# A decoder's second attention: the rotary jobs' scaling moved from VectorE to ScalarE, the table added in one instruction

## What is computed

```python
q = _layernorm(q, qn_g, qn_b)
k = _layernorm(k, kn_g, kn_b)
cos, sin = _rope_tables(s, D, ROPE_BASE)
q = q * cos + _rotate_half(q) * sin
k = k * cos + _rotate_half(k) * sin
...
scores = jnp.einsum('bhqd,bhkd->bhqk', q, k) / jnp.sqrt(jnp.float32(D))
scores = jnp.where(causal, -jnp.inf, scores)
weights = jax.nn.softmax(scores, axis=-1)
attn = jnp.einsum('bhqk,bhkd->bhqd', weights, v)
```

## Time and profile before

| | us |
|---|---|
| median of 3 runs | 946.5 (942.33 to 947.36) |
| profiled execution: time | 946.95 |
| profiled execution: span of the core | 945.2 |
| score slots 0 to 57 of attention 1 | 365.9 to 683.3 |

### The profile page before, as it was taken

The page is one execution under the profiler, slowest core; times in us unless marked ns, Lnnn a source line. Parts: engine busy times, 40 slices in busy tenths (PEclk is TensorE's granted clock), DMA queues, the critical chain, the costliest instruction groups (busy, mean ns, idle before and its releaser), DMA issues.

```text
span 945.2 us, 11992 instructions
## 1 busy us (share of the span) xinstructions
PE 777.5 (82%) x3984; PEld 563.8 (60%) x3984; DVE 695.0 (74%) x1067; ACT 473.2 (50%) x990; POOL 269.0 (28%) x178
## 2 busy tenths in 40 slices
PE   6761568867898976999988888989883799999997
PEld 2341446654343743676666656666662589999996
DVE  4879699889758977898999769869928644444443
ACT  1653467722255014566676547556763344444442
POOL 1000356522230121011010201201003366666663
PEclk9685679988899999999999989999996899999999
DMA  4313134325020220111111110103000053444341
GB/s 168 120 40 142 67 110 135 112 90 211 3 92 23 90 89 0 45 45 45 46 45 46 45 45 24 66 27 109 2 1 0 7 189 133 141 156 136 133 134 44
DMA packets 24208, 74.60 MB, mean 79 GB/s; under 512 B 3120, under 2 KB 5696, under 8 KB 23776
## 3 DMA queue, kind: packets, MB, share of 16 engines
q1 hardware_dynamic: 23776, 71.51, 21.4%
q10 hardware_dynamic: 384, 2.49, 0.8%
HBM read 72.55 MB, written 1.44 MB: 78 GB/s over the span
## 4 chain that ended last, share of the span: by engine, by line
PE 51%; DVE 20%; ACT 13%; issue 13%; POOL 2%; DMA 0%; POOLq 0%; DVEq 0%; ACTq 0%; SPq 0%
PE ps L1561 8%; PE ps L1675 6%; PE ps L1676 6%; PE ps L1677 6%; DVE hS L917 5%; PE ps L1522 4%; PE ps L1640 4%; ACT dA L544 3%; PE ps L1541 3%; PE ps L1324 2%; PE ps L1628 2%; DVE ps L909 2%; PE ps L1316 1%; PE ps L1619 1%; DVE lnst L939 1%
## 5 line engine op out<-in xcount | busy, mean ns | idle before, releaser
L1324 PE MATMUL ps<-ident,hS 128*128 128x128 f32 x512 | 73.3, 292 | 56.4 <-POOL hS L391 31.1
L1295 DVE SCALAR_TENSOR_TENSOR arena<-ps,arena 128x1024 f32<-128x1024 f32 x32 | 39.2, 1225 | 102.1 <-ACT arena L783 93.1
L917 DVE TENSOR_TENSOR_SCAN hS<-dA,hS 128x1024 f32<-128x1024 f32 x41 | 93.7, 2286 | 23.7 <-ACT dA L544 23.3
L1324 PEld LDWEIGHTS ps<-ident,hS 128*128 128x128 f32 x512 | 62.1, 150 | 77.0 <-POOL hS L391 38.1
L1561 PE MATMUL ps<-WB,hT 128*128 128x512 f32 x192 | 91.6, 623 | 3.8 <-DVE arena L1170 2.0
L419 POOL TENSOR_SCALAR jst<-jst 128x8 f32<-128x8 f32 x20 | 12.3, 613 | 276.7 <-DVE jst L1178 276.7
L391 POOL TENSOR_TENSOR hS<-hS,BCb 128x1024 f32<-128x1024 f32 x23 | 56.1, 2439 | 111.1 <-DVE ps L909 96.1
L544 ACT ACTIVATE dA<-DEL,negA 128x510 f32<-128x510 f32 x128 | 85.0, 720 | 4.7 <-DVE hS L917 4.3
L433 POOL TENSOR_TENSOR MHl<-arena,MHh 128x1024 fp32r<-128x1024 f32 x34 | 81.7, 2404 | 17.0 <-ACT MHh L786 17.0
L1675 PE MATMUL ps<-Wh,MHh 128*128 128x256 f32 x272 | 77.9, 286 | 5.8 <-POOL MHl L433 5.8
L1676 PE MATMUL ps<-Wl,MHh 128*128 128x256 f32 x272 | 77.6, 285 | 0.0
(11 more groups left out here) (223 smaller groups left out, 1885.1 us busy)
## 6 DMA issues: line engine op xcount, KB each, us to landing
BCb<-bc_dram SPq DMA_DIRECT2D x64, 512.0 KB, 3.7
arena<-gate_dram SPq DMA_DIRECT2D x32, 512.0 KB, 3.6
WB<-in_we SPq DMA_DIRECT2D x34, 256.0 KB, 2.7
WB<-in_wqkv SPq DMA_DIRECT2D x1, 3072.0 KB, 12.8
WA<-in_wo ACTq DMA_DIRECT2D x1, 2048.0 KB, 7.6
WA<-in_ffn SPq DMA_DIRECT2D x1, 1408.0 KB, 8.0
pkb<-in_pk SPq DMA_DIRECT2D x2, 698.0 KB, 4.7
X<-in_x SPq DMA_DIRECT2D x1, 1024.0 KB, 7.6
```

Of the source, the lines that this page charges most:

```text
L917: v.tensor_tensor_scan(f(h), f(a), f(dbu(g)), 0.0, ALU.mult, ALU.add).then_inc(s["scan_done"], 1)
L1324: last = mm(ps[:, ACC_BANK + j // 2, 256 * (j % 2) + P * d:256 * (j % 2) + P * d + P], src[:, d, P * j:P * j + P], ident[:], start=(first ...
```

## The change

ScalarE multiplies job_a by the eight scales, in place, as a part of its own, "scale", which stands in rope's slot. VectorE's rope keeps only the addition of job_a and job_b, and a new part, "bias", adds the table to all heads in one instruction of 1024 columns, one slot later (in the first two jobs in the same slot). tr stays where it was. For the jobs (b+1, 1) rope comes two slots after proj instead of three. In the costs rope goes from 3.2 to 1.2 and bias is 1.2. The semaphore job_rope counts jobs, no longer eighths.

```diff
+            def job_scale(b, i):
+                j = JOB[b, i]
+                act.wait_ge(s["job_add"], j + 1)
+                act.wait_ge(s["job_rstd"], j + 1)
+                for t in range(2):
+                    for h in range(REP1):
+                        c = slice(D1 * h, D1 * h + D1)
+                        last = sc.mul(job_a(j)[:, t, c], job_a(j)[:, t, c], jst[:, j % 2, 2, REP1 * t + h:REP1 * t + h + 1])
+                last.then_inc(s["job_scaled"], 1)
...
                 dve.wait_ge(s["job_rot"], 3 * (j + 1))
                 v.tensor_tensor(job_a(j), job_a(j), job_b(j), ALU.add).then_inc(s["job_add"], 1)
-                dve.wait_ge(s["job_add"], j + 1)
-                dve.wait_ge(s["job_rstd"], j + 1)
-                for t in range(2):
-                    for h in range(REP1):
-                        c = slice(D1 * h, D1 * h + D1)
-                        v.scalar_tensor_tensor(job_a(j)[:, t, c], job_a(j)[:, t, c], jst[:, j % 2, 2, REP1 * t + h:REP1 * t + h + 1],
-                                               tabs[:, 3 * x + 2, t, :], ALU.mult, ALU.add).then_inc(s["job_rope"], 1)
+
+            def job_bias(b, i):
+                j, x = JOB[b, i], 0 if i else 1
+                dve.wait_ge(s["job_scaled"], j + 1)
+                heads = job_a(j).rearrange("p t (h d) -> p t h d", d=D1)
+                shift = tabs[:, 3 * x + 2, :, :].unsqueeze(2).broadcast_to([P, 2, REP1, D1])
+                v.tensor_tensor(heads, heads, shift, ALU.add).then_inc(s["job_rope"], 1)
...
             def job_tr(b, i, x):
                 j = JOB[b, i]
-                pe.wait_ge(s["job_rope"], 8 * (j + 1))
+                pe.wait_ge(s["job_rope"], j + 1)
...
-    def rope_job(slot, b, i, rope=3, tr=5):
+    def rope_job(slot, b, i, rope=3, tr=5, later=1):
...
         at(slot + rope, "rope", (b, i))
+        at(slot + rope, "scale", (b, i))
+        at(slot + rope + later, "bias", (b, i))
...
-    rope_job(-8, 0, 0, 2, 3)
-    rope_job(-7, 0, 1, 2, 3)
+    rope_job(-8, 0, 0, 2, 3, 0)
+    rope_job(-7, 0, 1, 2, 3, 0)
...
-            rope_job(u + 9, b + 1, 1, 3, 4)
+            rope_job(u + 9, b + 1, 1, 2, 4)
...
-    cost = {"rot": 2.6, "sum": 1.2, "rope": 3.2, "dbu": 1.2, "scan": 3.5}
+    cost = {"rot": 2.6, "sum": 1.2, "rope": 1.2, "bias": 1.2, "dbu": 1.2, "scan": 3.5}
...
-        plan += pick("wo1", "rope", "rot", "sum") + [p for p in now if p[0] != "da"]
+        plan += pick("wo1", "rope", "scale", "rot", "sum", "bias") + [p for p in now if p[0] != "da"]
```

More of the change, by code:

```diff
@@ L256, in build @@
             s0_mm s0_tanh s0_exp pv0_mm pv0_copied pv0_tr at0_den at0_ready a_tr_mm a_tr_act a_tr_dve o0_mm x_new fsc_ready gate_tanh gate_h gate_mm gate_t nega_exp nega_ready pt0_fill
-            f_mm f_tanh f_hid fd_mm wdn_ready w1_mean w1_centered tabs_ready job_mm job_sq job_rot job_sum job_rstd job_add job_rope
+            f_mm f_tanh f_hid fd_mm wdn_ready w1_mean w1_centered tabs_ready job_mm job_sq job_rot job_sum job_rstd job_add job_scaled job_rope
             job_tr_mm job_tr_copied v_mm v_copied s1_mm s1_max s1_exp s1_rc s1_norm pt1_mm pt1_copied pv1_mm at1_copied o1_mm
@@ L750, in _ @@
                     job_copy(*a)
+                elif kind == "scale":
+                    job_scale(*a)
                 elif kind == "exp":
@@ L1175, in job_sum @@
                 if j >= 2:
-                    dve.wait_ge(s["job_rope"], 8 * (j - 1))
+                    dve.wait_ge(s["job_rope"], j - 1)
                 dve.wait_ge(s["job_sq"], j + 1)
@@ L1215, in _ @@
                     job_rope(*a)
+                elif kind == "bias":
+                    job_bias(*a)
                 elif kind == "max":
```

## The result

The changed kernel takes 976.22 us (median, 974.58 to 977.14) against 946.93 of the kernel before in the same runs: ratio 1.0318, 95% interval 1.0282 to 1.0354, slower. The forecast was 966, range 945 to 984. The profiled execution took 977.14, its span is 975.3. Executions of the kernel before differ among themselves: over all its measurements here they took 941.7 to 949.0, at a mean granted clock between 0.919 and 0.931. So a stage time, which is read from one profiled execution, can be off by a few us.

What follows compares the result with a forecast made beforehand. ScalarE's in-order run, as long as TensorE's own work, was taken to leave no room in the score slots. 33.0 - 13.9 - 1.5 + 4.4 = +22, less 2 or 3 for accumulations, +19: 966 us, range 945 to 984.

Steps and rivals of the forecast that it cites:

- What bounds the stage: Attention 1's score slots: ScalarE's run from projection's end to output copy is as long as TensorE's work, 0.07 us apart.
- The price of a multiplication: ScalarE's eight per job: 0.30 us each overlapped, 2.4 us per job; 3.3 if not overlapped at all.
- VectorE's saving is off the path: VectorE gives back about 1.0 us per job, 20 us; beyond 1.5 us in the last slots, no time gained.
- The exposed slots: Score slots behind a scale: 14 x 2.4 us less 0.49 and 1.09, +32.0, with the tail slot +33.
- The pacing: Planner's new costs remove five of six scan waits for the exp: -13.9 us, plus -1.5 from VectorE in the last slots.
- The accumulations: The scan's accumulations fall oftener in slots where TensorE stands still, taking off 2 or 3 us.
- The prologue: Before the score slots: job 1's scale stands behind the values' copy, its transposes at 361.2 instead of 356.83, +4.4 us.
- The signs that were named: Among others: output-copy wait up some 25 us, L544 waits down to one or two, job 1's transposes at 361.
- The bias: VectorE's bias addition waits for ScalarE's scale near nothing and hides; without cover it would cost up to 1 us a job.
- VectorE as the bound: Faster rival: multiplications fit ScalarE's idle time, 20 us of VectorE leave the path: 927, or 915 without dA waits; chance 0.12.
- The draw by soaking up: Rival: delays vanish where VectorE is late anyway; half of 33 stays, 952, or 947 with two thirds soaked up; chance 0.15.
- The dearer case: Slower rival: dA waits persist in other slots, or bias wait holds VectorE 1 us in most jobs: 989; chance 0.13.

Runs made afterwards that it cites:

- the pair of 941.51 and 945.74 us: Both exps put ahead of the scan: in the kernel before with the new planner costs and slots, 941.51 us; in the changed kernel with scales ahead of the square, 945.74.
- one multiplication: Changed kernel with one of each job's eight multiplications kept, seven blocks unscaled, all waits kept: 943.26 us, ratio 0.9978.
- the new pacing: Kernel before with only the planner's new costs and slots, VectorE keeping the eight scale-and-add instructions: 939.76 us, ratio 0.9935.
- the old costs: Changed kernel with only the planner's cost line put back (rope 3.2, no bias cost): 989.14 us, ratio 1.0486.
- the faster kernels: Split kernels with one multiplication (943.26 us) or early scale and both exps ahead of the scan (945.74), set against old-rope kernels at 939.76 and 941.51.
- the place in the list: Changed kernel with ScalarE's multiplications moved ahead of the square or copy that waits for TensorE: 943.18 us, ratio 0.9979.
- one line of order: Kernel before with one planner line changed, both exps of the next scan step ahead of the scan, old costs: 937.03 us, ratio 0.9905.
- the kernel that has only the prologue mended: Changed kernel with only job 1's scale moved ahead of the value projection's copy in slot -5: 966.06 us, ratio 1.0237.

## Why the prediction was right, point by point

*What bounds the stage: right.* A run of ScalarE as long as TensorE's own work, with 0.07 us between them, was read from one slot; the stall of 2.39 us stands exactly there. The slot was one without an accumulation, the kind with the least room. Of the normalisations behind a scale in the stage, none waits for VectorE any more.

*The price of a multiplication: right.* 2.35 us per job from first start to successor, 2.4 said.

*VectorE's saving is off the path: right, and shown* by the pair of 941.51 and 945.74 us, and by one multiplication at 943.26 against the new pacing's 939.76: less work on VectorE, and no gain.

*The exposed slots: right in kind, sized a little high.* The sum had +33 for the slots, the tail slot included, all of it time in which TensorE stands still. With the old costs the split adds 27.2 us of that. It also adds 8.3 us of busy time at a lower clock, for which the sum had no term: +35.5 together. On top of the new pacing it adds 29.0 (308.5 to 337.5): 19.5 of idle time and 9.5 of busy time.

*The pacing: near in size by luck.* The sum had -13.9 and -1.5. The -13.9 are the scans' waits for the exp, "taken whole". By itself the pacing took 9.0 us off these waits and 8.8 off the stage, yet TensorE's idle time did not fall (36.3 to 36.8). What fell was its busy time, by 9.4, most of it by a higher clock. With the scale on ScalarE the pacing gives -15.4, but that is 8.2 of busy and 7.1 of idle time, and most of the 7.1 are the accumulations. The step "I take it whole, because the stretches of chain around those waits run through the scan" was thus not borne out: the size came out near by other means.

*The accumulations: right in kind, sized too small.* The sum had 2 or 3. Seven more of the exposed slots carry one than with the old costs, and that takes off about 6 us.

*The prologue: mis-sized.* +4.4 was said, with bounds 2 to 5; it was +7.2. The first transposes come 14.68 us after the first projection, against 12.68 before: the 2.0 that was said. The second ones come 26.87 after it, against 21.33: +5.5 where 4.4 was said, because the first transposes and the value projection ran slower after a longer idle time of TensorE (1.97 and 5.72 us against 1.37 and 5.05). The projection behind the second ones took 5.04 us instead of 3.60, after an idle time of 4.70: the granted clock was 0.50 from 365.80 to 368.00, where before it was 1.00 from 356.83 to 361.20. The sum has no term for that. It carried each delay on as its own length and nothing more, and this is the step of this term that failed.

Together: the forecast's +19 was 15 for the stage and 4 for the prologue, and 20.2 and 7.2 were measured. Spans differ by 30.1, because 2.3 more lie ahead of the first projection, where the instructions are the same and the profiles of all kernels here differ by up to 4.1 us, and 0.5 behind slot 58. The medians differ by 29.3. So the mechanism, a stall behind the scale, is the foretold one; that the total came as near as it did owes something to luck, since the clock had no term and the pacing's term stood for something else.

*The signs that were named.* VectorE's waits for L544 are down to two. TensorE's wait for the output copy rose by 18.6 us, not by some 25, as ten of the stalls are partly filled by accumulations. The transposes of job 1 come at 364.63, not at 361.

*The bias: mostly hidden.* VectorE waited 12.9 us for the scale in ten jobs, at most 3.1, where "near nothing" was said; TensorE hardly waited for the bias in the stage. In the faster kernels the split costs some 3.5 to 4 us. Part of the 3.5 is the prologue, and the bias may be a part of both; no run isolates it.

*The rivals.* VectorE as the bound fell with 976. The draw by soaking up fell with the time as well. ScalarE's wait for the reciprocal did fall, but the new pacing alone takes it from 30.5 to 15.1, and behind the scale itself no normalisation waited and TensorE stood still. The dearer case said 989, and the old costs give 989.14; the scans' waits for the exp are indeed kept there (18.8 us), but the forecast's size for it left out the clock. The faster rival's second figure should be 913 by its own terms (947 less 20 less 13.9), not 915.

*The rule on occupancy* (the Trainium skill, "Perfetto Trace Analysis", Identifying the Most-Contended Engine: the most contended engine is the one with the highest occupancy) did not point at what pays. That page does not go by busy matmuls for TensorE but by its weight loads, which are busy for 64% here, or by the rate it reaches, so by the rule VectorE, at 88%, was the engine to relieve. It was relieved by 14 us, and the time rose by 20.

## What to carry to other kernels

Where queues run in order, read the gap between two engines' runs in one slot, not their busy shares: an engine that is 63% busy may have no room behind a given instruction and plenty in front of another. Before moving work to an idle engine, find out what its idle time waits for and put the work ahead of that wait; here the place in the list was worth 33 us. When a change carries a side effect in a planner, run that alone: here it was the only gain, and one line of order gets at least as much. And when a stage gets shorter, look whether the bounding engine stood still less or ran at a higher clock: here a gain of 8.8 us came with no less idle time, and mostly by the clock.

## What was not expected of the hardware

**TensorE's granted clock is a price of stalls.** In the prologue of the kernel after TensorE stood still for 4.70 us, and the next 8 matmuls of a projection took 5.04 us; without such a stall, in the kernel that has only the prologue mended, they take 3.60. The granted clock was 0.50 from 365.80 to 368.00, the lower of its two levels (1.2 and 2.4 GHz); transposes take 1.97 us at it and 1.04 at the higher. In the stages of the kernel after, of the one with the old costs and of the one with only the prologue mended, TensorE stood still behind a scale 19 times for 2.39 us and 21 times for 1.52. A stretch with a granted clock of 0.50 followed ten of the 19 and none of the 21. In the stage the price shows in the table of the old costs: 281.2 and 289.4 us for the same matmuls.

**GpSimd's product and VectorE's hold each other up.** In the timeline of the kernel with the scale on GpSimd:

```profile
473.41 2.28 DVE L931 TENSOR_TENSOR_SCAN hS<-dA,hS 128x1024 f32<-128x1024 f32 x1
...
473.64 3.75 POOL L424 TENSOR_TENSOR arena<-arena,jst 128x1024 f32<-128x1024 f32 x1 [3.55 <-DVE arena L1197]
...
475.73 2.74 DVE L938 TENSOR_TENSOR hS<-hS,BCb 128x1024 f32<-128x1024 f32 x1
...
487.60 1.22 DVE L938 TENSOR_TENSOR hS<-hS,BCb 128x1024 f32<-128x1024 f32 x1
```

GpSimd's product begins during the scan and ends at 477.39, 1.70 us after the scan; VectorE's product begins at 475.73 and ends at 478.47, 1.08 us after GpSimd's. In the prologue (348.42) GpSimd takes 1.90 us, beside products of VectorE that read one of their two inputs from PSUM, and VectorE's product without GpSimd takes 1.22. The times fit each waiting for the other to end and then taking about its own time; spans on GpSimd are rough. The Trainium skill ("SBUF — State Buffer", Who interferes with whom) says that these two engines share a port pair under an exclusive lock, and that a VectorE instruction with two SBUF inputs contends with a GpSimd instruction that reads SBUF; this trace agrees. Work on SBUF that goes to GpSimd beside a busy VectorE can be paid for on VectorE: here 16.8 us for 18 products.
